# Stationary operands of three bf16 matmul groups are read 128 columns wide instead of 112 or 125

## The reference, cut to what matters

```python
# second block: each of 8 experts takes the 224 tokens of 1792 that score highest
k = int(bs * CAPACITY) // n
scores = jax.nn.softmax(xf @ gate_w.T, axis=-1)
vals, idx = jax.lax.top_k(scores.T, k)
y = xf[flat_idx].reshape(k, n, d)
...
xf = xf.at[flat_idx].add(out.reshape(k * n, d))
# third block: softmax attention, 16 heads of 16
scores = jnp.einsum('bhqd,bhkd->bhqk', Q, K) / scale
weights = jax.nn.softmax(scores, axis=-1)
attn = jnp.einsum('bhqk,bhkd->bhqd', weights, V)
```

## Time and profile before

| | us |
|---|---|
| median of 3 runs | 758.5 (757.16 to 760.49) |
| span of the profiled execution | 756.5 |
| PE busy | 713.2 (94%) |
| PE weight loads busy | 605.2 (80%) |
| DVE busy | 501.1 (66%) |
| ACT busy | 337.7 (45%) |
| POOL busy | 294.2 (39%) |

### The profile page before, as it was taken

How to read it: one execution, slowest core, us unless ns; L and a number is a source line. 1 busy time by engine, 2 the same in 40 slices (tenths; PEclk the granted TensorE clock), 3 DMA queues, 4 the chain that set the end, 5 groups by cost and what they waited for, 6 DMA issues and landing times.

```text
span 756.5 us, 16705 instructions
## 1 busy us (share of the span) xinstructions
PE 713.2 (94%) x6469; PEld 605.2 (80%) x6469; DVE 501.1 (66%) x1259; ACT 337.7 (45%) x691; POOL 294.2 (39%) x224
## 2 busy tenths in 40 slices
PE   5899999989999999999998999999999898999998
PEld 4678788855588888888885777778777787899998
DVE  4888888886852243310468788787888767767565
ACT  2122222147734122221676778777787452323323
POOL 2333333528831333321434787877868100000000
PEclk9999999988999999999999999999999999999999
DMA  9977000016947955551553797786871000000000
GB/s 308 383 178 52 24 25 25 26 37 188 206 125 155 235 160 170 163 164 25 111 120 69 149 173 160 156 159 145 159 134 19 2 1 13 1 25 1 25 10 29
DMA packets 65610, 81.54 MB, mean 108 GB/s; under 512 B 32018, under 2 KB 55154, under 8 KB 64226
## 3 DMA queue, kind: packets, MB, share of 16 engines
q1 hardware_dynamic: 62434, 72.68, 40.7%
q0 software_dynamic: 2816, 3.67, 2.6%
q10 hardware_dynamic: 288, 4.19, 1.4%
HBM read 60.45 MB, written 19.31 MB: 105 GB/s over the span
## 4 chain that ended last, share of the span: by engine, by line
PE 68%; DVE 17%; issue 4%; DMA 4%; ACT 3%; POOL 2%; SPq 0%; DVEq 0%; POOLq 0%; ACTq 0%
PE psum L1187 7%; PE psum L852 6%; PE psum L1172 6%; PE psum L2451 5%; PE psum L2150 5%; DVE mx L1948 5%; PE psum L1617 5%; PE psum L185 4%; PE psum L2112 3%; PE psum L342 3%; DVE rsum L1971 3%; PE psum L2173 2%; PE psum L2137 2%; PE psum L884 2%; PE psum L1625 2%
## 5 line engine op out<-in xcount | busy, mean ns | idle before, releaser
L1948 DVE TENSOR_REDUCE mx<-psum 112x2 f32<-112x750 f32 x128 | 113.4, 926 | 13.2 <-PE psum L2112 12.7
L1857 ACT ACTIVATE probs<-psum 125x448 f32<-125x448 f32 x192 | 90.9, 545 | 29.6 <-PE psum L2137 29.5
L852 PE MATMUL psum<-w_parts,c_parts 128*125 128x512 f32 x288 | 74.1, 409 | 9.3 <-DVE w_parts L620 7.4
L1755 POOL TENSOR_TENSOR half_sum<-probs 125x896 f32<-125x896 f32 x30 | 62.8, 2092 | 38.8 <-ACT probs L1857 38.8
L2137 PEld LDWEIGHTS psum<-qpk,kpk 128*125 128x125 bf16 x768 | 61.5, 139 | 16.8 <-issue 8.2
L852 PEld LDWEIGHTS psum<-w_parts,c_parts 128*125 128x125 f32 x288 | 53.4, 189 | 23.9 <-DVE w_parts L620 7.4
L2137 PE MATMUL psum<-qpk,kpk 128*125 128x112 bf16 x768 | 67.5, 226 | 4.1 <-ACT probs L1857 3.1
L2112 PE MATMUL psum<-kpk,qpk 96*112 96x375 bf16 x256 | 62.3, 335 | 6.2 <-DVE mx L1948 4.7
L1761 POOL TENSOR_TENSOR tile_sum<-half_sum,probs 125x896 f32<-125x896 f32 x30 | 62.6, 2085 | 2.4
L1187 PE MATMUL psum<-we,hT 128*112 128x256 f32 x256 | 61.6, 403 | 0.0
L1030 ACT ACTIVATE hT<-psum,b 128x224 f32<-128x224 f32 x64 | 25.2, 444 | 79.0 <-PE psum L1172 78.3
(11 more groups left out here) (234 smaller groups left out, 1497.5 us busy)
## 6 DMA issues: line engine op xcount, KB each, us to landing
we<-in_we SPq DMA_DIRECT2D x6, 2048.0 KB, 8.9
kparts_d<-kp SPq DMA_DIRECT2D x16, 562.5 KB, 5.3
kpk<-kparts_d SPq DMA_DIRECT2D x16, 562.5 KB, 6.5
ctx_all<-in_ctxT SPq DMA_DIRECT2D x16, 375.0 KB, 4.5
kpk<-kparts_d SPq DMA_DIRECT2D x16, 375.0 KB, 7.3
we<-in_we ACTq DMA_DIRECT2D x2, 2048.0 KB, 12.4
kpk<-kparts_d SPq DMA_DIRECT2D x16, 187.5 KB, 4.0
qparts_d<-qp SPq DMA_DIRECT2D x16, 168.0 KB, 3.4
```

Of the source, the lines that this page charges most:

```text
L852: ins = pe.matmul(banks[B_KV[t]][0:KT, :], parts_of[:, x, k, t * KT:(t + 1) * KT], w_parts[:, k, w], start=(k == 0 and (x, w) == SPLIT[0]) ...
L1755: pool.tensor_tensor(half_sum[:, m], probs[:, m, 0], probs[:, m, 1], ALU.add)\
L1857: act.activation(probs[:, m, t, g * HU * SQ:(g + 1) * HU * SQ], banks[B_ST[u % 3]][0:KT, 0:HU * SQ], ACT.Exp, scale=SCALE)\
L1948: dve.tensor_reduce(mx[:, n % 2, H + 2 * j:H + 2 * j + 2], psum[0:SQ, first:first + 2, 0:SK], AX.X, ALU.max)\
```

## The change

The three stationary operands are read 128 columns wide. The moving operands, their number of columns, the count of instructions and their order on every engine stay as they were. The output of each of these matmuls has 128 rows instead of 112 or 125; nobody reads the rows that are added. So that the last tile of a slot may be read past its end, `onehot` and `qpk` get 16 more columns a slot and `kpk` 4, and DVE sets these to zero once (three small memsets: one ahead of the first one-hot rows, two at the start of the second attention). The columns read beyond a tile are otherwise those of its neighbour: the next half or sequence in `onehot`, the next head in `qpk`, the next key tile or head in `kpk`. A head's keys take 375 elements of two bytes and a tile of them 125, so that every second tile starts at an address that is not a multiple of four bytes.

```diff
+WIDE = 128
...
-    onehot = sb(ctx, "onehot", [SQ, 2, B, CAP], BF16)
+    onehot_wide = sb(ctx, "onehot", [SQ, 2, B * CAP + WIDE - SQ], BF16)
+    onehot = onehot_wide[:, :, 0:B * CAP].rearrange("p s (b c) -> p s b c", c=CAP)
...
-    kpk = sb(keys_ctx, "kpk", [128, AHEAD, H, SK], BF16, side="right")
+    kpk_wide = sb(keys_ctx, "kpk", [128, AHEAD, H * SK + 4], BF16, side="right")
+    kpk = kpk_wide[:, :, 0:H * SK].rearrange("p s (h k) -> p s h k", k=SK)
...
+        dve.memset(onehot_wide[:, :, B * CAP:], 0.0)
         dve.wait_ge(tabs_in.sem, tabs_in.at(2, 0))
...
-                    ins = pe.matmul(banks[B_IDX][0:SQ, h * (2 + NR):(h + 1) * (2 + NR)],
-                                    onehot[:, s, b, h * SQ:(h + 1) * SQ], token5[:, b * E0 + e],
+                    at = b * CAP + h * SQ
+                    ins = pe.matmul(banks[B_IDX][0:WIDE, h * (2 + NR):(h + 1) * (2 + NR)],
+                                    onehot_wide[:, s, at:at + WIDE], token5[:, b * E0 + e],
                                     start=(b == 0), stop=(b == B - 1))
...
-    qpk = sb(root, "qpk", [128, AHEAD, H, SQ], BF16)
+    qpk_wide = sb(root, "qpk", [128, AHEAD, H * SQ + WIDE - SQ], BF16)
+    qpk = qpk_wide[:, :, 0:H * SQ].rearrange("p s (h q) -> p s h q", q=SQ)
...
         dve.memset(mx[:], 0.0)
+        dve.memset(kpk_wide[:, :, H * SK:], 0.0)
+        dve.memset(qpk_wide[:, :, H * SQ:], 0.0)
...
-                ins = pe.matmul(banks[B_S[j % 2] + h][0:SQ, 0:SK], qpk[0:ROWS, s, 2 * j + h],
+                at = (2 * j + h) * SQ
+                ins = pe.matmul(banks[B_S[j % 2] + h][0:WIDE, 0:SK], qpk_wide[0:ROWS, s, at:at + WIDE],
                                 kpk[0:ROWS, s, 2 * j + h], start=True, stop=True)
...
-                ins = pe.matmul(banks[B_ST[u % 3]][0:KT, c * SQ:(c + 1) * SQ],
-                                kpk[:, s, h, t * KT:(t + 1) * KT], qpk[:, s, h], start=True, stop=True)
+                at = h * SK + t * KT
+                ins = pe.matmul(banks[B_ST[u % 3]][0:WIDE, c * SQ:(c + 1) * SQ],
+                                kpk_wide[:, s, at:at + WIDE], qpk[:, s, h], start=True, stop=True)
```

## The result

The changed kernel takes 748.7 us (median of 5 runs, 746.15 to 750.11); the kernel before, run beside it, 757.7 us (757.16 to 760.49). The ratio is 0.9845 [0.9813, 0.9876]: faster by 1.2 to 1.9%, some 11.7 us of 758.5, where 7.3 us were forecast. The two medians alone differ by less, 9.0 us or a ratio of 0.988, which lies outside that interval; by them the time is 748.7 us, inside the range. The same kernel was run once more among the experiments, beside 11 runs of the kernel before: 749.07 us, ratio 0.9864 [0.9833, 0.9895], with 10.8 us between the medians. So the gain is known to some 9 to 12 us.

A forecast was written before the change was run, and what follows sets the result against it. PE bounds the token search nearly throughout; the second attention's chain alternates between DVE and PE. Search 3.6 + attention 2.1 - memsets 0.1 + clock 1.7 = 7.3 us off 758.5 gives 751.2 us, range 747 to 755.5.

The forecast's parts named there:

- rivals 1, 3 and 4: 1: keys gain nothing, chance 0.12; 3: width only costs, 760 us, 0.06; 4: wide odd-start reads much dearer, slower, 0.03.
- Rival 2: Token search: finds stay at 45 ns a pair instead of 28, total 754 to 755.5 us; chance 0.07.
- written-out finds: Token search, experts 0 to 3: 1.6 us of pairs go to 0.9, taken as 0.8 us less each.
- the late ones: Finds of experts 5 to 7: only 16 pairs without register instructions gain, 0.4 us each, 1.2 us in all.
- a step: Second attention: 0.10 us less in each of 14 middle steps (0.07 four key pairs, 0.03 score head), 1.4 us.
- `shift_turn`: Second attention: it still waits for DVE's last maximum, so faster loads of the eight key pairs before it gain nothing.
- the falls of the clock: Half-clock stretches behind finds of experts 5 to 7, 1.7 us each; one of three taken as gone.
- between the two kinds: Long finds become 1.9 to 2.1 us, between those followed by a fall (2.3) and those not (1.6 to 1.8).
- the forecast's other terms: All but the clock: token search 3.6 us, second attention 2.1 us, less 0.1 us for memsets.
- The two gains that were "lost": Finds of experts 2 and 3 gain 0.8 us each, lost because PE then waits longer for expert 2's weights.
- Expert 4's find: First find in the loop, register instructions run ahead: 0.8 us less; a longer wait leaves them still more time.
- the first sequence: Start of second attention, taken as PE's alone: 24 pairs gain 12 ns, 12 others 8.5 ns, 0.4 us.

The follow-up runs named there:

- e1: The change with only the one-hot rows read 128 wide, keys and queries at old widths, pads kept; ratio 0.9894 to the kernel before, 752.4 us.
- e8: The change with queries read at 112 columns again, keys and one-hot rows still 128 wide; 748.3 us in one profiled run.
- e10: The change once more, unaltered, beside further runs of the kernel before; 749.1 us, ratio 0.9864.
- e5: The kernel before, loads still 112 columns, each find matmul streaming 96 moving columns instead of 5; 752.9 us, ratio 0.9893.
- e6: The change with sixteen more wide pairs of 5 columns behind each find; 757.8 us, ratio 0.9956 to the kernel before.
- e2: The change with only keys and queries read 128 wide, one-hot rows at 112; 757.9 us, ratio 0.9964 to the kernel before.
- e3: The kernel before with only the change's wider tiles and memsets, all reads at old widths; 761.2 us, ratio 1.0029.
- e7: The change with the find's loops over halves and sequences exchanged, halves inside; 745.6 us, ratio 0.9806 to the kernel before.

## Why the prediction was right or wrong

**Right.** Exactly 128 columns make the load quick, for keys at odd starts too, and rivals 1, 3 and 4 fall with the 96 to 100 ns of the rows and the 11.73 us of a step. Rival 2 falls with 25 ns a pair, below the 28 taken. The written-out finds were to gain 0.8 us and gained 0.8, the late ones 0.4 and gained 0.46, a step 0.10 and gained 0.10; `shift_turn` stayed with DVE, the pads cost nothing that a piece of the chain shows. The mechanism was right; the total was too small by 4.3 us of the two spans, and two terms were mis-sized: the falls of the clock, and what the finds of experts 2 to 4 gain at the weights.

**The clock, the step that failed most.** The prediction said "I take one of the three falls as gone", 1.7 us. All three went, 5.1 us. The find was placed by its length alone, "between the two kinds", with nothing to say on which side of the line 1.9 us lies; e1, e8, e10 and the change show it on the full-clock side in each of their profiles, e5 that the length is harmless once columns stream, e6 that the falls come back when the finds are lengthened. Length alone is not the rule either: the prediction's "five finds of 1.6 to 1.8 us had no such fall behind them" holds for its own profile, but e2 and e3 have a fall behind one of 1.79 us, and e2 none behind one of 2.34. Nor did the term see the falls as a thing that differs from one execution to the next. Over its 29 runs the kernel before spent 28 us at half clock on the mean, between mean granted clocks of 0.989 (755.4 us) and 0.973 (763 to 767 us); the change spent 16 and 21 us. At a third to a half of the difference, 2.5 to 6 us of the gain are clock over many executions, for 1.7 forecast. The rest, 6 to 8 us, is near the 5.6 us of the forecast's other terms and the 0.4 to 1.3 that the next point adds.

**The two gains that were "lost".** The prediction said that PE's "wait grows from 0.3 to 1.9 us" behind a transfer that lands only 1.6 us earlier. The wait was 0 in the profile of the change, 0.7 us in e8 and 1.0 us in e10. In e10 the find of expert 1 ended 2.4 us earlier than before, 0.7 of it from the clock ahead of the search, and the weights landed 2.7 us earlier (262.68 against 265.34); in the change 2.2 us and at least 3.8. The loads of keys that share the transfer engines took 24.0 us in the profile of before, by the first and last of their packets, and 21.6 to 23.3 us in the others, e5 with the old slots among them (23.2): a landing from one profile, 0.3 us from a tie, was treated as a fixed point. The other half of the same coupling was also missed. Expert 4's find was priced at 0.8 us less whatever PE waited. Its register instructions seem to run ahead only while PE waits: with a wait of 0.7 to 1.0 us it takes 0.79 us (e8, e10), with none 1.77, and of the narrow finds 1.67 with the wait of 0.3 and 2.2 with none (e2, e3). So what is saved at the wait is partly paid at the find, and by the start of the transposes behind it the two executions differ by 0.7 us only (269.32 and 270.02). Together these pieces gave 3.7 us in the first profile and 2.8 in e10, for 2.4.

**Small ones.** Up to the end of the first sequence 0.9 us were lost instead of 0.4 gained, for the most part since its stretch of half clock was 6.8 us long in this execution (3.4 us in e10). The prediction also took the sequence to be PE's alone. From the start of its `qpk` activations in the chain to the pair of maxima behind its normalisation it takes 16.44 us in the profiles without half clock there, with narrow keys (e1, e5) and with wide ones (e2), and the chain then runs through two sums on POOL: there the loads gain nothing. With 3.4 us of half clock it takes 16.77 before, 16.65 in e10 and 16.57 in e6, with 6.8 us 17.79 in e3 (narrow) and 17.33 in the change. So a single stretch of 3.4 us costs 0.1 to 0.3 us here, where behind a find it costs 1.69. Why the falls at the two ends of the second attention come and go was not settled, nor why the first block has 3.4 us of half clock in one execution and 10.2 in another.

## What to carry to other kernels

Price a stationary read by the distance between pairs in a stream, not by the length of a load, and if it isn't fp32 see whether it can be read at exactly 128 columns; the neighbour's columns will do where nobody reads the extra rows, and 127 gives nothing. Look at what runs behind a phase of many loads and few moving columns: its price can be the half clock of the work that follows, and streaming more columns through the same loads can buy it back without any load getting quicker. What a stretch of half clock costs depends on where it lies, and where it lies changes between executions, so take the clock from many of them. A wait that one profile shows within a few tenths of a tie is neither a bound nor free; take both ends, and follow what the wait itself hides, here the register instructions of the next find.

## What the runs showed that was not expected

- A find that streams 96 columns instead of 5 is as long as before, within 0.06 us, and the kernel with it is 7 us quicker (e5).
- A step of one column, 127 to 128, takes a pair from 58 to 25 ns; from 112 to 127 it rises from 50 to 58.
- The kernel before spends between 17 and 41 us at half clock in different executions, and its time goes with that, from 755.4 to 766.7 us over 29 runs, though not with that alone: at one and the same 27 us its spans still lie between 754.5 and 758.1 us.
- The order of two loops around 32 pairs is worth 0.4 us in a find of the loop, of which the transposes behind it give back a third (e7).
- The same 3.4 us of half clock cost 1.69 us behind a find and 0.1 to 0.3 us in the first sequence of the second attention.
